# Gathering the upper rows of the pair list one stage earlier, and packing a list two groups behind

## The reference

```python
x = _layernorm(x + L0(x))   # relu(x[src] + edge_attr), summed over dst, plus (1 + eps) x
x = _layernorm(x + L1(x))   # 10 steps of f = 0.9 * segment_sum(f[src] * weight, dst) + 0.1 * x
x = _layernorm(x + L2(x))   # per edge type: relu(x W1 + b1) W2, times norm, summed over dst, relu
x = _layernorm(x + L3(x))   # max over the edges of a node of theta (x[dst] - x[src]) + phi x[src]
```

## Time and profile before

| | |
|---|---|
| median of three runs | 4958.19 us |
| the profiled execution | 4952.22 us, of which the span 4950.1 us |
| TensorE, VectorE busy | 2892.4 us (58%), 3047.2 us (62%) |
| GpSimd (POOL), ScalarE busy | 2596.0 us (52%), 1261.6 us (25%) |
| mean granted TensorE clock | 0.731 of full speed |

### The profile page before, as it was taken

One profiled execution on the slowest core, in us unless ns is written; L12 is line 12 of the kernel. 1 busy time (PEld: TensorE's weight loads), 2 busy tenths in 40 slices (PEclk: granted clock), 3 DMA queues, 4 the chain that ended last, 5 costly groups with the idle time before them and its releaser, 6 DMA issues. The chain is left out here.

```text
span 4950.1 us, 60862 instructions
## 1 busy us (share of the span) xinstructions
PE 2892.4 (58%) x9882; PEld 1516.2 (31%) x9882; DVE 3047.2 (62%) x7896; ACT 1261.6 (25%) x3891; POOL 2596.0 (52%) x2528
## 2 busy tenths in 40 slices
PE   4700000577776999999999566656222210897665
PEld 3500000233332666666666211111111100333332
DVE  8989990788886777777777444433233326564333
ACT  0133330232332444444444111111100002342111
POOL 0067777555552233333333477747465560565776
PEclk9955555777777999999999688778555555997555
DMA  2067762899998454444444255533333324232111
GB/s 65 0 176 216 217 206 50 139 148 149 147 146 145 130 136 131 130 135 128 134 133 128 68 142 145 140 68 64 56 48 48 46 36 113 65 73 49 38 38 27
DMA packets 735672, 526.54 MB, mean 106 GB/s; under 512 B 526161, under 2 KB 647962, under 8 KB 730594
## 3 DMA queue, kind: packets, MB, share of 16 engines
q1 hardware_dynamic: 582822, 381.10, 30.2%
q0 software_dynamic: 92160, 102.50, 14.2%
q10 hardware_dynamic: 60612, 42.15, 4.0%
HBM read 270.21 MB, written 261.82 MB: 107 GB/s over the span
## 5 line engine op out<-in xcount | busy, mean ns | idle before, releaser
L1224 POOL DMA_INDIRECT out<-xob,ob x400 | 426.6, 1067 | 813.0 <-DVE xob L1327 716.5
L486 POOL DMA_INDIRECT xdst<-in_x,dstc x400 | 457.4, 1143 | 402.1 <-PEq L634 260.7
L270 POOL DMA_INDIRECT gb<-nodes,ib x400 | 393.2, 983 | 289.2 <-ACT ib L841 190.0
L259 PE MATMUL bank<-ident,act 128*99 128x128 f32 x400 | 87.1, 356 | 767.9 <-DVE act L985 698.5
L283 PE MATMUL bank<-l_chosen,l_rec 128*3 128x512 f32 x480 | 310.1, 807 | 119.3 <-DVE l_chosen L277 119.3
L290 PE MATMUL bank<-chosen,rec 128*6 128x512 bf16 x1200 | 377.9, 481 | 1.5 <-DVE chosen L277 1.5
L270 POOL DMA_INDIRECT cgb<-layer,ib x160 | 176.1, 1100 | 252.4 <-ACT ib L2102 205.2
L259 PEld LDWEIGHTS bank<-ident,act 128*99 128x99 f32 x400 | 66.4, 224 | 775.6 <-issue 775.6
L1249 PE MATMUL bank<-hm,w 128*112 128x512 f32 x600 | 301.1, 640 | 0.0
L264 PE MATMUL bank<-ident,scan 99*128 99x99 f32 (+2 forms) x1120 | 198.8, 307 | 145.6 <-DVE scan L1915 101.9
L1266 PE MATMUL bank<-bxT,w 121*128 121x512 f32 x600 | 276.5, 597 | 11.9 <-ACT bxT L1176 11.9
(11 more groups left out here) (296 smaller groups left out, 7468.3 us busy)
## 6 DMA issues: line engine op xcount, KB each, us to landing
nodes<-wt SPq DMA_DIRECT2D x40, 1286.2 KB
edges<-gb ACTq DMA_DIRECT2D x100, 194.0 KB
run_rows<-tb SPq DMA_DIRECT2D x100, 194.0 KB, 6.3
xa<-run_rows SPq DMA_DIRECT2D x100, 194.0 KB, 3.3
kb<-edge_keep SPq DMA_DIRECT2D x100, 192.0 KB
lsb<-edges SPq DMA_DIRECT2D x200, 96.0 KB
deep_sum<-bzeros SPq DMA_DIRECT2D x50, 384.0 KB
layer<-bzeros SPq DMA_DIRECT2D x50, 384.0 KB
```

Of the source, the lines that this page charges most:

```text
L259: last = nc.tensor.transpose(slot(dst_ps[0:w, :], t), rows_sb[:, t, c0:c0 + w], ident[:, :])
L270: yield nc.gpsimd.indirect_dma_start(out=dst[s][:, t, 0:width], out_offset=None, in_=table, in_offset=bass.IndirectOffsetOnAxis(ap=ib[s][: ...
L486: nc.gpsimd.indirect_dma_start(out=xdst[:, k * F:(k + 1) * F], out_offset=None, in_=a["x"], in_offset=bass.IndirectOffsetOnAxis(ap=dstc[:, ...
L1224: nc.gpsimd.indirect_dma_start(out=out, out_offset=bass.IndirectOffsetOnAxis(ap=ob[s][:, t:t + 1], axis=0), in_=xo[s][:, t, :], in_offset= ...
```

## The change

A new DRAM table `upper_rows` holds a copy of the first 97 columns of `run_rows`, with rows of just that width; the first edge stage stores each `tb` tile twice. The second edge stage loads `xa` from it. It also loads the parents' numbers (row 0 of `lists`), turns them into integers on ScalarE, gathers the parents' 97 columns from `upper_rows` on GpSimd ahead of its scatter, and stores them in list order in the new table `parent_rows`. It does so for all of its 100 groups. Level 0 loads `gp` from there with one plain DMA and gathers only `gr`. In levels 0 and 1 `pack_up` runs two groups behind instead of one, `unpack` three instead of two, `store_list` four instead of three, and `rec` has four buffers instead of two.

```diff
@@ first edge stage: SyncE store, and the waits on tb
                         sp.dma_start(cells(run_rows, g, 1, 0, PW), tb[b][:, :, :]).then_inc(s_tbw[b], 16)
+                        sp.dma_start(cells(upper_rows, g, 1, 0, PW), tb[b][:, :, :]).then_inc(s_tbw[b], 16)
-                        wait(act, s_tbw[b], 16 * (i * 2 + s // 2))
+                        wait(act, s_tbw[b], 32 * (i * 2 + s // 2))
@@ second edge stage, SyncE
-                        sp.dma_start(xa[s][:, :, :], cells(run_rows, g, 1, 0, PW)).then_inc(s_xa[s], 16)
+                        sp.dma_start(xa[s][:, :, :], cells(upper_rows, g, 1, 0, PW)).then_inc(s_xa[s], 16)
+                    def load_numbers(i, s):
+                        g = i * U + s
+                        wait(sp, s_pi, g - U + 1)
+                        sp.sem_inc(sp_turn, 1)
+                        sp.dma_start(parent_no[s][:, :], lists[0:1, bass.ds(g * GE + 1, GE)].rearrange("o (p t) -> (o p) t", t=T)).then_inc(s_pn[s], 16)
+                    def store_parents(i, s):
+                        g = i * U + s
+                        sp.wait_ge(s_pg[s], (i + 1) * 16 * T)
+                        sp.sem_inc(sp_turn, 1)
+                        sp.dma_start(rows(parent_rows, g), flat(parent[s])).then_inc(s_pw[s], 16)
                         part(load, i, s, 0, end)
+                        part(load_numbers, i, s, 0, end)
...
                         part(store_x3, i, s, 4, end)
+                        part(store_parents, i, s, 5, end)
@@ second edge stage, ScalarE (between copy_x and the square of layer 2)
+                    def number(i, s):
+                        act.wait_ge(s_pn[s], (i + 1) * 16)
+                        wait(act, s_pg[s], i * 16 * T)
+                        nc.scalar.copy(ib[s][:, 0:T], parent_no[s][:, :]).then_inc(s_pi, 1)
@@ second edge stage, GpSimd
+                    def fetch(i, s):
+                        pool.wait_ge(s_pi, i * U + s + 1)
+                        wait(pool, s_pw[s], 16 * i)
+                        pool.sem_inc(pool_turn, 1)
+                        for ins in gather(s, upper_rows, parent, PW):
+                            ins.then_inc(s_pg[s], 16)
+                    def body(i, s):
+                        fetch(i, s)
+                        scatter(i, s)
-                    turns(pool, scatter)
+                    turns(pool, body)
@@ level
-            gathers = 2 * T if k == 0 else T
+            gathers = T
+            packs = 2 if U == 4 else 1
-                gp = st("gp", width, U)
+                gp = st("gp", PW, U)
-                msg, lt, rec = st("msg", wm), st("lt", PW), st("rec", 3)
+                msg, lt, rec = st("msg", wm), st("lt", PW), st("rec", 3, U)
+                            if k == 0:
+                                sp.sem_inc(sp_turn, 1)
+                                sp.dma_start(flat(gp[s]), rows(parent_rows, g)).then_inc(s_gp[s], 16)
-                                part(store_list, i, s, late, end)
+                                part(store_list, i, s, packs + 2 if U == 4 else late, end)
-                                part(unpack, i, s, 2, end)
+                                part(unpack, i, s, packs + 1, end)
-                            for ins in gather(s, table, gp, width):
+                            for ins in gather(s, table, gr if k == 0 else gp, width):
                                 ins.then_inc(s_g[s], 16)
-                            if k == 0:
-                                for ins in gather(s, table, gr, width, T):
-                                    ins.then_inc(s_g[s], 16)
-                                part(pack_up, i, s, 1, end)
+                                part(pack_up, i, s, packs, end)
```

More of the change, by code:

```diff
@@ L136, in gnn @@
         held = dram("held", (EP, 2 * F))
+        upper_rows = dram("upper_rows", (EP + 1, PW))
+        parent_rows = dram("parent_rows", (EP + 2 * GE, PW))
         first_sum = dram("first_sum", (EP, F))
@@ L1097, in gnn @@
             s_o = [sem(f"b_o{s}") for s in range(U)]
+            parent_no, parent = slots("parent_no", [P, T], scope=scope), st("parent", PW, U)
+            s_pg = [sem(f"b_pg{s}") for s in range(U)]
+            s_pn, s_pw = ([scope.sem(f"b_{n}{s}") for s in range(U)] for n in ("pn", "pw"))
+            s_pi = scope.sem("b_pi")
             (s_ones, s_cols, s_xT, s_h, s_h1, s_m, s_mw, s_scan2, s_scan3, s_rows, s_rc, s_d, s_dT, s_th,
@@ L1152, in body @@
                         part(store_x3, i, s, 4, end)
-                    drained(sp, body, 4)
+                        part(store_parents, i, s, 5, end)
+                    drained(sp, body, 5)
                     sp.wait_ge(s_fill, 16 * NG)
                     for s in range(U):
-                        for done in (s_x2w, s_rtw, s_x3w):
+                        for done in (s_x2w, s_rtw, s_x3w, s_pw):
                             sp.wait_ge(done[s], 16 * NT)
@@ L1508, in body @@
                             if k < 2:
-                                part(store_list, i, s, late, end)
+                                part(store_list, i, s, packs + 2 if U == 4 else late, end)
                         load(0, 0)
                         load(0, 1)
-                        drained(sp, body, late, n)
+                        drained(sp, body, packs + 2 if U == 4 else late, n)
                         for b in range(2):
@@ L1583, in body @@
                             if k < 2:
-                                part(unpack, i, s, 2, end)
+                                part(unpack, i, s, packs + 1, end)
                         stage(0, 0)
                         stage(0, 1)
-                        drained(act, body, 2, n)
+                        drained(act, body, packs + 1, n)
                     @block.gpsimd
@@ L1645, in pack_up @@
                             pe.sem_inc(pe_turn, 1)
-                            pack(psC[b], rec[b], chosen[b], 3).then_inc(s_pack, 1)
+                            pack(psC[b], rec[s], chosen[b], 3).then_inc(s_pack, 1)
                         def sums(i, s):
@@ L1657, in body @@
                             if k < 2:
-                                part(pack_up, i, s, 1, end)
+                                part(pack_up, i, s, packs, end)
                             part(sums, i, s, 0, end)
-                        drained(pe, body, 1, n)
+                        drained(pe, body, packs, n)
                     @block.vector
```

24 lines of the change are left out of this document (14 added, 10 removed).

## The result

The changed kernel takes 4795.4 us (median of four runs, 4792.3 to 4797.0), the kernel before on the same chip 4958.4 us. The ratio is 0.967, with the interval 0.965 to 0.969: 163 us less. Forecast were 4813 us with the range 4768 to 4895.

The account below looks back on a forecast made before the run. Level 0 was taken to be bound by GpSimd's gathers. Level 0 -161, second edge stage +11 and first edge stage +5 sum to -145 us: 4952.22 to 4807, with the median 6 us above, 4813 us; 80% range 4768 to 4895.

Parts of the forecast that it names:

- The bound of level 0: Level 0: GpSimd sets the pace, 10.34 us a group, with eight gathers of 0.95 + 0.3 us making 10.0.
- Level 0's new pace: Level 0: 6.4 us a group instead of 10.34, with 30% at half clock; -161 us in all, bounds -195 and -75.
- The pack's shift: Level 0: without packing two groups behind, packs, sums, copies and run_end run in series, some 7.7 us at full clock.
- Level 1: Level 1: GpSimd keeps four gathers and four scatters a group, so the packs' shift changes 0 us, bounds -5 and +5.
- Second edge stage: Second edge stage: GpSimd's 10.6 us fits under the 11.53 period; +3 us over 100 groups, +8 at the end, bounds 0 and +70.
- GpSimd's reads beside VectorE: Second edge stage: moved gathers lie beside VectorE's two-input instructions; one scatter so held took 1.85 us instead of 0.98.
- (d): Second edge stage: every gather held like that scatter, GpSimd at 14.1 us a group, +260 us, total 5070 us; chance 5%.
- First edge stage: First edge stage: 100 more stores, ScalarE waiting a few tenths for tb in some groups; +5 us, bounds 0 and +94.
- (a): First edge stage: DMA engines, 94% busy, are full; half to all of its bound, +70, total 4878 us; chance 10%.
- (b): Second edge stage: gathers lose 0.4 us each, GpSimd becomes the bound at 12.2 us a group, +65, total 4878 us; chance 10%.
- (c): Pair stage: stays near 8.5 us a group through half clock or SyncE's wait order; gain 74, total 4897 us; chance 6%.
- (e): Second edge stage: 60 empty groups' gathers of one row land late, ScalarE's number stalls, +120, about 4935 us; chance 3%.

Follow-up runs that it names:

- Experiment 6: Changed kernel with pack_up one group behind again in levels 0 and 1, on a usual chip: 4913.5 us, ratio 0.990 to the kernel before.
- experiment 8: Changed kernel with the load of gp and the store of held issued by ScalarE instead of SyncE: 4783.7 us, ratio 0.964 to the kernel before.
- Experiment 7: Changed kernel with the parents' loads, gathers and stores stopped after 52 of the second edge stage's 100 groups: 4787.5 us, ratio 0.965.
- experiment 10: Changed kernel with a fifth gather per group in the second edge stage, into a buffer nobody reads, on a usual chip: 4875.9 us, ratio 0.985.
- experiment 11: Changed kernel with four tb buffers instead of two in the first edge stage: 4788.1 us, ratio 0.967 to the kernel before.
- experiment 9: Kernel before with only the change's edits to the two edge stages, level 0 untouched, on a usual chip: 4967.1 us, ratio 1.0025.
- experiment 1: Changed kernel with pack_up one group behind again, on the chip where the kernel before takes 5317.5 us: 5637.7 us, ratio 1.060.
- experiment 2: Kernel before with only the packing moved to two groups behind in levels 0 and 1, on the slow chip: 5288.5 us, ratio 0.995.
- experiment 3: Kernel before with only the change's edits to the two edge stages, level 0 untouched, on the slow chip: 5798.4 us, ratio 1.090.
- experiment 4: Changed kernel with a fifth gather per group in the second edge stage, on the slow chip: 5751.9 us, ratio 1.083.

## Why the prediction was right, and where not

**The bound of level 0, right.** Half of GpSimd's gathers gone, the group fell from 10.5 to 6.1 us and `message` waits for `gr` once instead of 29 times. Experiment 6, with the gathers gone and the shift undone, is still faster than before.

**Level 0's new pace, right in kind, 18 us off in size.** Forecast -161, measured -3.4 - 170.9 - 4.5 = -178.8. Of the 18 us, 40 x (6.4 - 6.14) = 10 are the pace. The term that was mis-sized is the clock: I had 30% of the time at half. Over the whole stage the granted clock is 0.93, which by the two levels is 14% at half, and 1 / (0.86/5.9 + 0.14/8.5) = 6.17 us, nearly the 6.14 measured. I had taken a value between level 0 of before and the 0.92 of the second edge stage; with TensorE busy in 191 of 240 us the stage came out at the second. Most of the rest is the drain (the last groups of the stage), where I had +2 and the marker shows -4.5; which part of it became shorter was not followed. That SyncE is tightest at full clock was half right: experiment 8 gained 0.4 us a group by relieving it, but the waits are landings, of `first_sum` and `held`, and not the issues alone. I had `held` "within 3 us" and 20 us of room; the issue of 2950.73 is followed 4.1 us later by the gather that it releases. GpSimd runs ahead of the message, which my count from the message left out. For the forecast it cost little, 28.2 us of waiting on an engine with room.

**The pack's shift, right in mechanism, too small in price.** I gave 7.7 us a group without it, "at full clock". Experiment 6 shows the series as described and 9.14 us: the packs shown take 5.29 us, not 3.6, after 3.4 us of idle TensorE, and 7.7 + 1.7 = 9.4. Had I carried the clock into that sentence, I would have come near it.

**Level 1, right.** Forecast 0, measured -2.2.

**Second edge stage, right.** Forecast +3 for the period and +8 for the end; measured +0.8 and +9.0, of which 3.4 come back because level 0's first message needs four gathers less. GpSimd's time a group was forecast at 10.6 us: 143.3/17.35 groups = 8.26, and eight issues of 0.3 are 2.4, 10.7 in all. Experiment 7 takes half of the gathers away and the period does not move. One slip: I placed ScalarE's `number` of four groups later in the body of the `xob` that it follows. It runs one group behind the body, so the wait has one period more of room than I gave it. The stalls that I priced at 3 us are not there.

**GpSimd's reads beside VectorE, right in kind.** Scatters of up to 1915 ns stand in the tile view above, so single instructions are held up as the 1.85 us one was the earlier trace rows. Together they weigh little: the moved gathers take 980 ns on average by the page (392.0 us for 400), the gathers of `gp` in level 0 before took 976 (156.2 us for 160), and the scatters went from 1067 to 1096. That is 4 x (4 + 29) ns = 0.13 us a group, where rival (d) needed 0.6 us on each gather. None of the 400 moved gathers took more than 1.43 us: the long ones are scatters, and it was the gathers that I had feared for. A scatter of 1.90 us at 2200.44 lies beside the scan of two SBUF inputs that runs from 2200.27 to 2201.55, and ends 0.8 us after it, as the one before did. The Trainium skill, "SBUF — State Buffer", section "Who interferes with whom", which I cited, says that a VectorE instruction with two SBUF inputs contends with a GpSimd instruction that reads SBUF. The single long scatters agree with it; what such waits add up to over a stage it does not give.

**First edge stage, right in size, the path not shown.** Forecast +5, measured +7.5. The wait that I had named is there (38 times, 60.1 us), but experiments 10 and 11 show that the stage's time does not follow it: 667.8 us with 192.6 us of such waits, 669.6 with none. What the 7.5 us are stays open; they are less than the profiles of this stage differ among themselves.

**The rivals.** (a), DMA engines full, is refuted wherever the kernel before takes its usual time: "94% busy" at 147 GB/s gave 178 GB/s when asked. (b) and (d), GpSimd as the bound, are refuted by experiments 7 and 9, and (c) by the pace. (e), late gathers of row 0, was the nearest to being true: they take four times the DMA time, and at five a group they cost 80 us (experiment 10), with waits in ScalarE's `number` (85.9 us), the place that I had written. At four no wait for them shows.

**What stays open.** On the chip of experiments 1 to 4 the changed edge stages cost 481 us, and from the sum of the parts the changed kernel would probably be slower there than the kernel before (an estimate: 5317 + 481 - 210 = some 5590, with 523 us for level 0 in experiment 2 and 313 in experiment 4; experiment 1 is 5638). That is more than any rival had, and the nearest rival in kind, (a), does not describe it: waits for landings last up to 14 us while the DMA engines are half idle. Why on this chip, the runs do not say. Which wait holds level 0 at 5.9 us was not pursued either; four buffers for the sum that `first_sum` stores would be the next thing, and were not tried.

## What to carry to other kernels

Work can be moved onto a busy engine of another stage at almost no cost if that stage is bound by something else without a gap: compare the group's time on the engine that takes the work with the stage's period (here 10.7 us against 11.5), and then price the drain, where the cover is gone (9 us). When one engine's work is halved, ask which series of dependences comes up next, and at which clock. Here the loop packs, sums, copy, one-hots would have kept 112 of 171 us. Before a stage's few microseconds are put down to one wait, compare the same stage in the other profiles. And measure on more than one chip before a kernel is given more concurrent transfers.

## What the runs showed of the hardware that I had not expected

- **A DMA share near 1 is not a full DMA.** 0.94 at 147 GB/s became 1.09 at 178 GB/s, and the stage grew from 671 to 678 us. A share above 1 can only come about if the time of packets is counted that overlap.
- **Gathers that all read one row take four times the DMA time** of gathers with distinct rows: some 76 against 18 engine-us for 512 rows of 388 bytes (79 and 21 with the scatters of the same queue), at equal packets and bytes a group. An "empty" group is dearer than a full one.
- **Chips differ with the load.** On one chip the kernel before takes 7% more, and the added traffic costs 481 us; on another 13 us. The second edge stage without the moved gathers is the same on both, 1141 us (experiment 2): there that stage is slowed only once the change has added its transfers. Level 0 is slow on that chip already without them, 13.4 us a group against 10.5.
- **The clock rose as the waits went.** Over the whole of level 0 TensorE was granted 0.80 with 61% of the time busy (the kernel before), 0.81 with 65% (experiment 6), 0.93 with 80% (the changed kernel) and 0.94 with 81% (experiment 8). In experiment 8 one stretch of 100 us reached full clock:

```profile
2950.00:3050.00 100.00, 85.89 (x285) 28.94 (x285) 88.29 (x284) 29.32 (x122) 74.94 (x71) 1.00 0.89 224
```
